# Head and tail written out in orders of their own in a two-layer graph-attention kernel

## The reference

```python
v, q, k = (relu(x @ W + b) for W, b in ((Wv, bv), (Wq, bq), (Wk, bk)))
scores = q @ k.T                                     # 1024 x 1024 a graph
att = softmax(scores * mask - 9e15 * (1 - mask))     # mask = adj
x = layernorm(x + relu((att @ v) @ Wo + bo))
h = x @ W_w.T + W_b
u = mask * exp(e[:, None] + f[None, :] + a_b)        # e = h @ a1, f = h @ a2
x = layernorm(x + (u / u.sum(axis=2)) @ h)
```

## Time and profile before

| | |
|---|---|
| median of 3 runs | 442.85 us (437.96, 442.85, 443.32) |
| the profiled execution | 437.73 us, its span 436.0 us |
| mean granted TensorE clock | 0.976 |
| busy in the span | PE 403.1, DVE 325.7, ACT 306.9, POOL 260.6 us |
| DMA | 80.72 MB, mean 185 GB/s |

### The profile page before, as it was taken

One profiled execution on the slowest core, in us unless ns is written; L12 is line 12 of the kernel. 1 busy time (PEld: TensorE's weight loads), 2 busy tenths in 40 slices (PEclk: granted clock), 3 DMA queues, 4 the chain that ended last, 5 costly groups with the idle time before them and its releaser, 6 DMA issues.

```text
span 436.0 us, 8669 instructions
## 1 busy us (share of the span) xinstructions
PE 403.1 (92%) x2918; PEld 375.8 (86%) x2918; DVE 325.7 (75%) x929; ACT 306.9 (70%) x569; POOL 260.6 (60%) x223
## 2 busy tenths in 40 slices
PE   3989999999999999999999999999999999997740
PEld 2769998999999999999999999999999999996640
DVE  2377589767887978877887978877887979888631
ACT  3586768786878778686878778686878677775510
POOL 3763572556247772869447772869447752751955
PEclk9999999999999999999999999999999999999685
DMA  6573264647381737476383737476373737246521
GB/s 231 183 244 128 93 207 142 265 135 251 101 336 48 255 133 275 160 245 238 100 337 97 260 127 266 171 252 231 104 283 98 251 135 239 102 146 210 180 95 48
DMA packets 36684, 80.72 MB, mean 185 GB/s; under 512 B 2592, under 2 KB 19104, under 8 KB 36640
## 3 DMA queue, kind: packets, MB, share of 16 engines
q1 hardware_dynamic: 36352, 79.70, 53.7%
q10 hardware_dynamic: 288, 0.46, 0.3%
HBM read 75.96 MB, written 4.19 MB: 184 GB/s over the span
## 4 chain that ended last, share of the span: by engine, by line
PE 85%; POOL 5%; DVE 4%; DMA 2%; ACT 1%; issue 1%; POOLq 0%; DVEq 0%; ACTq 0%
PE m_ps L927 12%; PE pt_ps L876 12%; PE av_ps L888 7%; PE av_ps L890 7%; PE av_ps L889 7%; PE s_ps L823 7%; PE s_ps L825 6%; PE s_ps L824 6%; PE m_ps L825 6%; PE m_ps L824 6%; PE m_ps L823 6%; PE m_ps L905 2%; DMA adjt_in<-in_adj_t_dram 1%; DMA xt_in<-in_x_t_dram 1%; DVE prob L577 1%
## 5 line engine op out<-in xcount | busy, mean ns | idle before, releaser
L585 DVE TENSOR_TENSOR prob_tl<-pt_ps,prob_th 128x512 fp32r<-128x512 f32 x128 | 84.4, 682 | 24.5 <-ACT prob_th L416 24.4
L577 DVE CUSTOM_DVE_ANT_0 prob<-s_ps,penalty 128x1024 f32<-128x1024 f32 x64 | 78.0, 1219 | 24.0 <-PE s_ps L825 22.2
L416 ACT ACTIVATE prob_th<-pt_ps 128x512 fp32r<-128x512 f32 x128 | 73.0, 592 | 28.4 <-PE pt_ps L876 28.3
L369 ACT ACTIVATE adj_t<-adjt_in 128x1024 fp32r<-128x1024 f32 x64 | 67.1, 1056 | 25.1 <-PE m_ps L927 15.4
L408 ACT ACTIVATE prob<-prob,neg_max 128x1024 f32<-128x1024 f32 x64 | 73.8, 1153 | 10.9 <-DVE neg_max L577 10.6
L927 PE MATMUL m_ps<-g,adj_t 128*128 128x258 f32 x512 | 76.3, 295 | 4.5 <-DVE g L648 1.9
L876 PE MATMUL pt_ps<-ident,prob 128*128 128x128 f32 x512 | 73.7, 273 | 0.0
L888 PE MATMUL av_ps<-prob_th,vh 128*128 128x256 f32 x256 | 73.6, 287 | 0.0
L927 PEld LDWEIGHTS m_ps<-g,adj_t 128*128 128x128 f32 x512 | 67.3, 195 | 6.0 <-ACT adj_t L369 3.4
L890 PE MATMUL av_ps<-prob_th,vl 128*128 128x256 f32 x256 | 72.4, 283 | 0.0
L889 PE MATMUL av_ps<-prob_tl,vh 128*128 128x256 f32 x256 | 72.4, 283 | 0.0
(11 more groups left out here) (99 smaller groups left out, 879.0 us busy)
## 6 DMA issues: line engine op xcount, KB each, us to landing
adj_in<-in_adj_dram SPq DMA_DIRECT2D x64, 512.0 KB, 4.3
adjt_in<-in_adj_t_dram SPq DMA_DIRECT2D x64, 512.0 KB, 4.2
xt_in<-in_x_t_dram SPq DMA_DIRECT2D x8, 512.0 KB, 6.8
x_in<-in_x_dram SPq DMA_DIRECT2D x8, 512.0 KB, 4.7
out_dram<-out_sb SPq DMA_DIRECT2D x16, 256.0 KB, 4.5
wb<-in_pack_b_dram ACTq DMA_DIRECT2D x1, 320.0 KB, 6.3
wa<-in_pack_a_dram ACTq DMA_DIRECT2D x1, 132.0 KB, 4.5
```

The lines of the kernel that those rows point to most:

```text
L416: sc.activation(prob_th[n % 2][:, tiles(k), (i % 2) * P:(i % 2 + 1) * P], pt_ps[k][:, :].rearrange("p (c n) -> p c n", n=P), ACT.Copy).the ...
L577: v.tensor_tensor_reduce(out=prob[i % 2][:, :], in0=s_ps[:, :, :].rearrange("p a n -> p (a n)"), in1=penalty[:, n % RING, :], scale=-1.0, ...
L585: v.tensor_tensor(prob_tl[n % 2][at], pt_ps[k][:, :].rearrange("p (c n) -> p c n", n=P), prob_th[n % 2][at].bitcast(F32), ALU.subtract).th ...
```

## The change

Each engine's program is now a `head()` for batch 0, six middle passes `batch_pass(p)`, p = 1 to 6, and a `tail()` for batch 7 (`LAST`) and what is left of 5 and 6. All three are new lists of the same calls, the middle passes too. Beside the order:

- nine matmuls of the identity with itself (`warm_up`) open TensorE's program;
- x transposed is loaded in halves, and wb by SyncE behind the first two halves; ScalarE loads wa alone;
- the low parts of x, q and k of batch 0 are made by VectorE;
- in the last batch, layer 0's variance, power, normalization and g's denominators go by halves; its adjacency tiles 0 to 5 are rounded into `qh`, `ql`, `kh`, `kl`, `xth`, `xtl`; aggregations 0 to 4 accumulate in the banks of scores, transposes and attention, and the first four chunks of each are multiplied before the second half of g exists;
- the last batch's end goes by pairs of tiles: scale, residual and statistics on VectorE, the power on GpSimd, the normalization as scale and bias on ScalarE, four stores.

```diff
+        def adj_tile(b, i):
+            if b < LAST:
+                return adj_t[:, (T * b + i) % RING, :, :]
+            if i < 6:
+                return (qh, ql, kh, kl, xth, xtl)[i][:, :].rearrange("p (t d) -> p t d", d=P)
+            return adj_t[:, i - 6, :, :]
...
+        for i, ps in enumerate((s_ps[:, 0, :], s_ps[:, 1, :], pt_ps[0], pt_ps[1], av_ps)):
+            bank["agg", LAST, i] = ps
...
-            def load_x_t(b):
-                wait(sp, xtl_done, 2 * b)
-                sp.dma_start(xt_in[:, :], x_t[b]).then_inc(xt_arrived, 16)
+            def load_x_t(b, k):
+                if b > 0:
+                    sp.wait_ge(*lower(xtl_done, b - 1, k))
+                sp.dma_start(half(xt_in, k), half(x_t[b], k)).then_inc(xt_arrived[k], 16)
+
+            def load_wb():
+                sp.dma_start(wb[:, :], pack_b).then_inc(wb_arrived, 16)
...
+            def store_pair(g):
+                sp.wait_ge(out_last, 2 * g + 2)
+                sp.dma_start(out_dram[LAST][:, pair(g), :], out_sb[:, pair(g), :]).then_inc(stored_last, 16)
+
+            def head():
+                load_x_t(0, 0)
+                load_x_t(0, 1)
+                load_wb()
+                load_adj(0, 0)
+                load_x_t(1, 0)
+                load_adj(0, 1)
...
             def round_adj(b, i):
                 n = T * b + i
-                wait(act, agg_full, n - RING + 1)
+                if b < LAST:
+                    wait(act, agg_full, n - RING + 1)
+                elif i < 4:
+                    act.wait_ge(s_full, T * B)
+                elif i < 6:
+                    act.wait_ge(q_full, 2 * B)
+                    act.wait_ge(k_full, 2 * B)
+                    act.wait_ge(v_full, 2 * B)
+                else:
+                    act.wait_ge(agg_full, T * (LAST - 1) + i - 1)
                 act.wait_ge(adjt_arrived[n % STAGING], 16 * (n // STAGING + 1))
...
+            def norm1_pair(g_):
+                act.wait_ge(out_free[g_ // 2], 16 * LAST)
+                act.wait_ge(shift1_done, g_ + 1)
+                for t in range(2 * g_, 2 * g_ + 2):
+                    sc.activation(out_sb[:, t, :], gs[:, t, 0:D], ACT.Identity, bias=shift1[:, t:t + 1],
+                                  scale=rstd1[:, t:t + 1]).then_inc(out_last, 1)
...
-            nc.scalar.dma_start(wa[:, :], pack_a).then_inc(wa_arrived, 16)
-            nc.scalar.dma_start(wb[:, :], pack_b).then_inc(wb_arrived, 16)
...
+            def first_k_lo(k):
+                dve.wait_ge(kh_done, k + 1)
+                v.tensor_tensor(half(kl, k), half(kf, k), half(kh, k).bitcast(F32), ALU.subtract).then_inc(kl_done[0], 1)
...
+            def residual1_pair(g_):
+                dve.wait_ge(x1b_done, B + g_ // 2)
+                dve.wait_ge(scale1_done, B + g_)
+                for t in range(2 * g_, 2 * g_ + 2):
+                    v.scalar_tensor_tensor(out=gs[:, t, 0:D], in0=gs[:, t, 0:D], scalar=scale1[:, t:t + 1],
+                                           in1=x1b[:, t, :], op0=ALU.mult, op1=ALU.add).then_inc(r1_last, 1)
...
+            def shift_pair(g_):
+                dve.wait_ge(rstd1_done, B + g_)
+                v.scalar_tensor_tensor(out=shift1[:, pair(g_)], in0=mv1[:, pair(g_), 0], scalar=-1.0, in1=rstd1[:, pair(g_)],
+                                       op0=ALU.mult, op1=ALU.mult).then_inc(shift1_done, 1)
...
+            def aggregate_early(i):
+                if i == 0:
+                    pe.wait_ge(gl_den_done, B)
+                    pe.wait_ge(gl_done, TH * LAST + 2)
...
+                pe.wait_ge(adjt_done, T * LAST + i + 1)
+                sums(i, range(TH))
...
+            def warm_up():
+                pe.wait_ge(ident_ok, 2)
+                for _ in range(WARM):
+                    pe.matmul(pt_ps[0][:, 0:P], ident[:, :], ident[:, :], start=True, stop=True)
```

More of the change, by code:

```diff
@@ L240, in _ @@
+            head()
+            for p in PASSES:
                 batch_pass(p)
+            tail()
             for k in range(2):
-                sp.wait_ge(out_free[k], 16 * B)
+                sp.wait_ge(out_free[k], 16 * LAST)
+            sp.wait_ge(stored_last, 16 * TH)
         @block.gpsimd
@@ L356, in _ @@
+            constants()
             head()
-            for p in range(-1, B + 3):
+            for p in PASSES:
                 batch_pass(p)
+            tail()
         @block.scalar
@@ L557, in _ @@
+            sc.dma_start(wa[:, :], pack_a).then_inc(wa_arrived, 16)
+            head()
+            for p in PASSES:
                 batch_pass(p)
+            tail()
         @block.vector
@@ new lines, in head @@
+            def head():
+                split_qk()
+                first_x_lo(0)
+                first_x_lo(1)
+                split_vo()
+                first_k_lo(0)
+                first_q_lo(0)
+                first_k_lo(1)
+                v_out(0, 0)
+                place_rhs1()
+                v_out(0, 1)
+                mask_max(0, 0)
+                mask_max(0, 1)
+                first_q_lo(1)
+                prob_lo(0, 0, 0)
+                prob_lo(0, 0, 1)
+                split_w1()
+                mask_max(0, 2)
+                prob_lo(0, 1, 0)
+                prob_lo(0, 1, 1)
+                v_out(1, 0)
+                mask_max(0, 3)
+                prob_lo(0, 2, 0)
+                prob_lo(0, 2, 1)
+                mask_max(0, 4)
+                prob_lo(0, 3, 0)
+                prob_lo(0, 3, 1)
+                mask_max(0, 5)
+                prob_lo(0, 4, 0)
+                av_lo(0, 0)
+                mask_max(0, 6)
+                prob_lo(0, 4, 1)
+                prob_lo(0, 5, 0)
+                av_lo(0, 1)
+                prob_lo(0, 5, 1)
+                mask_max(0, 7)
+                prob_lo(0, 6, 0)
@@ L803, in batch_pass @@
-                if there(p - 1):
-                    av_lo(p - 1, 2)
-                if there(p - 3):
-                    var_eps1(p - 3)
-                if there(p):
-                    mask_max(p, 0)
-            split_weights()
-            place_rhs1()
-            for p in range(0, B + 3):
+                prob_lo(p - 1, 7, 0)
+                av_lo(p - 1, 2)
+                v_out(p, 1)
+                prob_lo(p - 1, 7, 1)
+                if there(p - 2):
+                    agg_out(p - 2, 0)
@@ L813, in _ @@
+            head()
+            for p in PASSES:
                 batch_pass(p)
-                if p == 0:
-                    split_w1()
+            tail()
         @block.tensor
```

1209 lines of the change are left out of this document (821 added, 388 removed), and 8 rows, old and new, of tables (PASS_SLOTS, SLOTS).

## The result

The changed kernel takes **457.66 us** (median of 4 runs, 454.94 to 461.46) against 442.21 us of the kernel before in the same comparison (4 runs, 437.96 to 443.32): ratio **1.042, 95% interval 1.036 to 1.048, slower**. The forecast was 425.5, range 417.5 to 433. The profiled execution took 458.06 us, its span is 456.0 against 436.0.

A forecast was written before the change was run, and what follows sets the result against it. TensorE was taken to be full in middle passes, with 44 us of the span at the ends. 436.0 + 1.0 - 3.2 - 2.5 - 7.8 + 0.3 gave 423.8, plus 1.7 gave 425.5 us; range 419 to 431, with rivals 417.5 to 433.

The forecast's parts named there:

- meeting of VectorE and GpSimd: Separate term of the sum: VectorE and GpSimd blocking each other adds 0.3 us to the span.
- The middle passes: Six passes in new order: TensorE stays full, tight waits at pass boundaries cost +1.0 us for all, bounds 0 and 3.
- Rival 3: Head and small tail steps: VectorE and GpSimd block each other, low parts of k and q slowed; +2, 427.5 us; chance 0.10.
- Rival 4: Middle passes: GpSimd's late residual delays k's low parts, up to 3.3 us in each of five passes; 442 us; chance 0.03.
- Rival 1: Middle passes: thin slacks make the boundary waits cost 1 us a pass; 430.5 us; chance 0.17.
- Rival 2: Head: pause behind the warm-up counts as rest, full pace only at 15.6 us as before; +2.8, 428.3 us; chance 0.10.
- the 1.3 of the forecast: Head: half-pace loss of matmuls from 6.0 to 8.6 us after the warm-up, 1.3 us, bounds 0 and 4.1.
- The head, -3.2: Start of kernel: earlier first product, half-pace loss and waits lose 11.2 us against 14.35; -3.2, bounds -5.5 and +0.5.
- The tail, -2.5 and -7.8: From last attention product to last matmul 26.8 us against 29.3, -2.5; behind last matmul 8.6 against 16.4, -7.8.
- my bound of 28.9: Tail: last matmul 28.9 us behind the last attention product if every adjacency load takes 4.4 us; 26.8 was forecast.
- my own sign of being wrong, 29: Tail: a last matmul beyond 29 us behind the last attention product would refute the forecast.
- the steps of pairs 0 to 2: Tail: steps of these tile pairs lie hidden under TensorE's last products, and would begin to show if adjacency came earlier.

The follow-up runs named there:

- experiment 8: On experiment 4, VectorE's SBUF-to-SBUF steps and GpSimd's work kept apart in pass 1 and tail too: 424.68 us, ratio to the kernel before 0.968.
- experiment 1: Changed kernel with layer 0's normalizations put ahead of scale_out in the six middle passes: 439.42 us, ratio to the kernel before 0.9998.
- experiment 4: On experiment 1, place_rhs1 moved ahead of k's low parts and the split of w1 divided and moved in the head: 432.42 us, ratio to before 0.986.
- experiment 9: On experiment 8, adjacency tiles 4 to 7 of the last batch loaded ahead into the four adj_in tiles: 425.07 us.
- experiments 10 and 11: Batch 6's statistics moved behind g's first low parts, 10 on experiment 9 and 11 on experiment 8: 426.21 and 426.72 us.

## Why the prediction was wrong

| part | forecast, against before | changed kernel | with the conflicts removed (experiment 8) |
|---|---|---|---|
| head and pass 1 | -3.2 | +1.3 | -8.8 |
| passes 2 to 6 | +1.0 (all six passes) | +16.7 | -0.7 |
| tail | -10.3 | +2.0 | -3.4 |
| meeting of VectorE and GpSimd | +0.3, beside | in the rows above | none |
| span | -12.2 | +20.0 | -12.9 |

The borders of this table are the first scores of batches 2 and 7. The new order does 16 matmuls (`project_out` of a half and one transposed half, 1.6 us) behind such a border that the old one did ahead of it. For equal work the first row reads +3.0 and -7.2, the third +0.4 and -5.0; passes 2 to 6 gain 16 matmuls and lose 16.

**The step that failed: "The middle passes ... I take a loss of +1.0 for all, bounds 0 and 3".** Measured: +16.7 us in passes 2 to 6 alone, 52.3 us a pass. I laid out the new order with the durations of the old one and checked each wait; the waits are right (experiment 1: 48.86 us a pass, none at the boundary). What I took over with the durations was the assumption that an instruction costs the same wherever it stands. For the normalization it does not: 341 ns apart from GpSimd, 718 on average in the new place. The bound of 0.5 us a pass was "the size of the slacks", not the size of what could lengthen: eight instructions that can take up to 1.2 us each. The sum had a term of its own for VectorE and GpSimd meeting, 0.3 us. It measured 17.3 us in passes 2 to 6 (experiment 1) and 6.4 us in pass 1 and tail (experiment 8).

**Rival 3 named the mechanism and put it in the wrong place.** It had the lock, the right rows and the cited rule, and priced it at +2 for the low parts of k and q in the head and small tail steps. It did not ask which other SBUF-to-SBUF steps of VectorE the new lists put beside GpSimd. The two lists said it: `scale_out` directly ahead of `norm0` on VectorE, and `residual1`, released by `scale_out`, next on GpSimd. The sum with what was measured: 1.0 + 15.7 more in passes 2 to 6.

**Rival 4** had the other half, the late residual of GpSimd, and asked only whether it delays k's low parts. It does not: k's first low part starts at 238.80 in experiment 1, 6.6 us after GpSimd has fallen idle. Its time of 442 and its mechanism both missed. **Rival 1**, boundary waits, is refuted. **Rival 2**, the clock: at the start not as written (first product at 6.63 with 0.47 us), yet the half rate came later, behind the waits at 14.5 and 29.1, and cost part of the 7 us of experiment 4. Its price was wrong as well: the half rate from 6.0 to 15.6 us would lose 4.8 us, 3.5 more than the 1.3 of the forecast and not 2.8.

**The head, -3.2.** The first product was well placed (6.0; 6.63, and 5.92 in experiment 8). The waits for place_rhs1 and the split of w1 were found (0.9 and 2.6; 2.22 and 2.73). Too small was what they entail: the half rate behind them, forecast nowhere in the head but at its start. With both gone head and pass 1 gain 7.2 us for equal work, 6.7 of them ahead of scores(1, 0), more than the upper bound of 5.5.

**The tail, -2.5 and -7.8.** Both were counted from the end of the last attention product, and what lies ahead of it I left at the old length. In the changed kernel it ends 58.4 us behind scores(7, 0), 57.4 in experiment 4, and 52.4 in experiment 8; in the old one 50.6, with 16 matmuls (1.6 us) less to do. Behind it, with equal work, came 39.9 us, and 40.4 in experiment 8, instead of 35.4; the old kernel took 45.7. The last matmul ended 30.3 us behind the attention product (31.7 in experiment 8), beyond my bound of 28.9 and my own sign of being wrong, 29. For the lower clock I had added nothing; it was granted at 0.50 over 9.6 us there, and how much of the 3.5 us too many is its share was not separated. The loads of the slabs, my bound for the last matmul, are late as I said, but experiment 9 shows that they do not set the end of the kernel: the end is VectorE's, 2.1 to 2.7 us a pair. I had put the steps of pairs 0 to 2 down as hidden and added that they would show if the slabs came earlier; they show already. The 8.6 us behind the last matmul were nearly right (9.6).

That experiment 8 lands at 424.68, 0.8 from the forecast, is in good part luck: for equal work the head and pass 1 gain 7.2 us where 3.2 were forecast, the tail 5.0 where 10.3 were.

Not settled: the worth of the warm-up (0 to 2.4 us), why the first products are slow in some executions with it, and how far the 1.2 and 1.9 us that experiments 10 and 11 lose in the tail, read from one trace each, hold in the median.

## What to carry to other kernels

When an order is rewritten, list for each stretch the SBUF-to-SBUF steps of VectorE beside what GpSimd does at that time, and ask what releases GpSimd; here a small VectorE step that starts GpSimd's long work was better placed behind VectorE's own SBUF work. In a trace the sign is one group of instructions whose mean has doubled while its count has not changed, and min/median/max far apart. A total that agrees with the forecast proves no term of it; compare stage by stage.

## What the runs showed that I had not expected

- How long a VectorE step gets beside GpSimd: in these rows it goes by the GpSimd instruction and not by the step's own size. Eight columns took 2.38 us beside a 2.36 us addition; a copy of 128x2 took 1.01 us at 8.12 in experiment 4, beside a conversion of 1.05 that began at 8.06. Eight normalizations beside a row of GpSimd instructions took 5.99 us.
- GpSimd loses too, though less: a conversion took 1.25 and a low part 1.69 us beside VectorE's low parts and copies in the changed kernel's head (1.04 and 1.28 alone).
- Steps of VectorE with one operand in PSUM kept their time beside GpSimd's residual: low part of x1 0.69 us at 399.56 in experiment 4. So did the statistics, which read one SBUF tile: 0.86 us for four at 402.86.
- The power on GpSimd takes 1.65 us for eight columns, 1.02 for four and 0.70 to 0.86 for two; I had assumed 1.65 for any.
